# A hint for the closing branches of two hardware loops, in a fused attention and expert block

## The reference

```python
def _L0_attn_ref(x, w_kv_down, w_kv_up, w_q, w_out):
    kv = (x @ w_kv_down) @ w_kv_up
    ...
    att = jnp.einsum('bqhd,bkhd->bhqk', q, k) * scale
    att = jax.nn.softmax(jnp.where(causal, att, -jnp.inf), axis=-1)
    y = jnp.einsum('bhqk,bkhd->bqhd', att, v)
    return y.reshape(Bx, Tx, HD) @ w_out
...
    scores = jax.lax.stop_gradient(feats @ centroids.T)
    expert = jnp.argmax(scores, axis=1)
    alpha = jax.nn.sigmoid(jnp.sum(feats * centroids[expert], axis=-1, keepdims=True))
    ys = jax.vmap(_sublayer, in_axes=(None, 0, 0, 0, 0, 0, 0))(feats, gamma, beta, W1, b1, W2, b2)
    out = alpha * y + (1.0 - alpha) * feats
...
    x = x + _layernorm(_L0_attn_ref(_layernorm(x), ...))
    x = x + _layernorm(_L0_ffn_ref(_layernorm(x), ...))
```

## Time and profile before

| what | value |
|---|---|
| median of three runs | 1459.13 us (1459.09 to 1460.83) |
| profiled execution, its own time | 1459.58 us |
| span of its instructions | 1457.7 us |
| TensorE busy | 1343.0 us, 92% |
| VectorE busy | 1234.4 us, 85% |
| ScalarE busy | 1083.2 us, 74% |
| GpSimd busy | 809.8 us, 56% |
| mean granted TensorE clock | 0.977 |

### The profile page before, as it was taken

One profiled execution on the slowest core, in us unless ns is written; L12 is line 12 of the kernel. 1 busy time (PEld: TensorE's weight loads), 2 busy tenths in 40 slices (PEclk: granted clock), 3 DMA queues, 4 the chain that ended last, 5 costly groups with the idle time before them and its releaser, 6 DMA issues.

```text
span 1457.7 us, 34718 instructions
## 1 busy us (share of the span) xinstructions
PE 1343.0 (92%) x9120; PEld 1210.6 (83%) x9120; DVE 1234.4 (85%) x4806; ACT 1083.2 (74%) x3186; POOL 809.8 (56%) x1216
## 2 busy tenths in 40 slices
PE   7999999999999999999999999999999999599993
PEld 6988898888888988888888888888888888488872
DVE  5899888888888888888888888888888887499994
ACT  5888787878787878788787878787878886366661
POOL 3445555555555555555555555555555554178886
PEclk9999999999999999999999999999999999699997
DMA  4000000000000000000000000000000000312120
GB/s 194 5 9 12 12 11 12 11 8 11 12 11 12 11 11 10 9 11 11 11 11 12 11 10 11 10 11 12 11 12 11 9 9 14 95 48 63 59 62 8
DMA packets 38793, 32.39 MB, mean 22 GB/s; under 512 B 4882, under 2 KB 35990, under 8 KB 38304
## 3 DMA queue, kind: packets, MB, share of 16 engines
q1 hardware_dynamic: 31968, 21.61, 4.9%
q0 software_dynamic: 4608, 8.67, 1.7%
q10 hardware_dynamic: 2112, 1.11, 0.3%
HBM read 20.35 MB, written 12.07 MB: 22 GB/s over the span
## 4 chain that ended last, share of the span: by engine, by line
DVE 46%; issue 22%; ACT 18%; POOL 6%; PE 5%; ACTq 1%; DMA 1%; DVEq 1%; POOLq 0%; SPq 0%
DVE nscore L851 15%; DVE p_lo L861 13%; ACT prob L722 10%; ACT t_hi L694 5%; DVE nmax L851 2%; POOL prob L1037 2%; DVE ff L367 2%; DVE hitr L891 2%; DVE wup_s L384 1%; DVE on L393 1%; POOL pay L1056 1%; DVE fn L793 1%; DVE gg L402 1%; DVE t_lo L838 1%; DVE rinv L832 1%
## 5 line engine op out<-in xcount | busy, mean ns | idle before, releaser
L1037 POOL TENSOR_TENSOR prob<-prob,rinv 128x256 f32<-128x256 f32 (+1 forms) x512 | 413.2, 828 | 507.8 <-DVE rinv L832 507.7
L722 ACT ACTIVATE prob<-nscore,nmax 128x128 f32<-128x128 f32 (+1 forms) x1024 | 458.7, 449 | 248.4 <-DVE nmax L851 248.4
L851 DVE CUSTOM_DVE_ANT_0 nscore<-psS,mask 128x128 f32<-128x128 f32 (+1 forms) x1024 | 319.9, 350 | 0.0
L861 DVE TENSOR_TENSOR p_lo<-psP,p_hi 128x768 fp32r<-128x768 f32 x256 | 243.7, 952 | 1.0 <-ACT p_hi L694 0.9
L838 DVE TENSOR_TENSOR t_lo<-psT,t_hi 128x512 fp32r<-128x512 f32 x256 | 175.9, 687 | 56.0 <-ACT t_hi L694 56.0
L607 PE MATMUL psP<-ident,prob 128*128 128x128 f32 x1536 | 216.4, 277 | 6.8 <-DVE p_lo L861 6.7
L694 ACT ACTIVATE p_hi<-psP 128x768 fp32r<-128x768 f32 x256 | 204.9, 800 | 1.6 <-PE psP L607 1.6
L579 PE MATMUL psS<-t_lo,xt_hi 128*128 128x256 f32 (+1 forms) x512 | 196.8, 384 | 0.0
L722 ACT ACTIVATION_READ_ACCUMULATOR prob<-nscore,nmax 128x1 f32 x1024 | 191.3, 187 | 0.0
L607 PEld LDWEIGHTS psP<-ident,prob 128*128 128x128 f32 x1536 | 167.2, 141 | 22.7 <-POOL prob L1037 8.8
L867 DVE TENSOR_TENSOR z_lo<-psZU,z_hi 128x512 fp32r<-128x512 f32 x256 | 175.7, 686 | 3.3 <-ACT z_hi L694 3.3
(11 more groups left out here) (167 smaller groups left out, 3246.0 us busy)
## 6 DMA issues: line engine op xcount, KB each, us to landing
fin<-routed_rows SPq DMA_DIRECT2D x40, 136.0 KB, 2.2
wx<-ffn_w SPq DMA_DIRECT2D x2, 2058.0 KB, 12.0
xin<-x SPq DMA_DIRECT2D x32, 128.0 KB, 2.1
xres<-x SPq DMA_DIRECT2D x32, 128.0 KB, 2.1
out<-res,fin POOLq DMA_INDIRECT x80, 2.3
routed_rows<-padr ACTq DMA_DIRECT2D x4, 272.0 KB, 4.3
routed_rows<-padr SPq DMA_DIRECT2D x4, 272.0 KB, 5.4
wup_s<-wup SPq DMA_DIRECT2D x1, 1024.0 KB, 4.9
```

Source lines behind the costliest of these rows:

```text
L722: last = nc.scalar.activation(prob[:, p1, h, a:z], nscore[:, h, a:z], ACT.Exp, bias=nmax[:, p1, h, q:q + 1], scale=-1.0, accum_out=rsum[:, ...
L851: last = v.tensor_tensor_reduce(nscore[:, h, a:z], psQ[q][:, h, :], mask[:, a:z], -1.0, -MASKED, ALU.add, ALU.min, nmax[:, p1, h, q:q + 1])
L861: v.tensor_tensor(p_lo[:, (s - 3) % 2], psP[:, :, 0:384], p_hi[:, (s - 3) % 2].bitcast(F32), ALU.subtract).then_inc(S["p_split"], 1)
L1037: last = g.tensor_tensor(pr, pr, rinv[:, p2, :, q:q + 1].broadcast_to([P, 2, z - a]), ALU.mult)
```

## The change

Both loops are made through a small helper which asks for the same loop, on the same engine, with the option `hint_back_edge=True`.

```diff
+        def hinted_loop(eng, first, end):
+            return nc.Fori(first, end, engines=bass.OrderedEngineSet([eng.engine]), hint_back_edge=True)
+
         def ffn_phases(eng, slot):

             for s in range(FU):
                 slot(0, 0, s, lambda lag: s >= lag)
-            with eng.Fori(1, TILES // FU) as it:
+            with hinted_loop(eng, 1, TILES // FU) as it:
                 m0 = eng.snap(it * FU)
                 n0 = eng.snap(it * 16)
                 for s in range(FU):
@@ -476,7 +479,7 @@
             for s in range(SLOTS):
                 slot(0, 0, s, lambda lag: s >= lag, lambda d: s // PAIRS >= d)
             if ITERS > 2:
-                with eng.Fori(1, ITERS - 1) as it:
+                with hinted_loop(eng, 1, ITERS - 1) as it:
                     g0 = eng.snap(it * SLOTS)
                     b0 = eng.snap(it * 2)
                     for s in range(SLOTS):
```

## The result

| | before | changed |
|---|---|---|
| median | 1459.11 us (1458.6 to 1460.83, 4 runs) | 1434.78 us (1434.12 to 1435.53, 4 runs) |
| profiled execution, its own time | 1459.58 us | 1435.53 us |
| span | 1457.7 us | 1431.8 us |
| mean granted clock | 0.977 | 0.983 |

The profiled execution has 3.7 us around its span, that of before 1.9 (the other three runs of the change have 3.0, 2.0 and 2.0); what that is stays open. The ratio is 0.9831, with a 95% interval of 0.9814 to 0.9848: the change makes the kernel 24.3 us faster. Forecast were 1432.5 us, in a range of 1430.5 to 1439.0. The median is 2.3 us above the forecast, just outside the 1430.5 to 1434.5 that the forecast itself covered, and in the band of the rival *exits are paid* (1434.4 to 1438.2).

A forecast was written before the change was run, and what follows sets the result against it. It took the round VectorE, ScalarE and back as pacing the kernel, with VectorE idle for a code fetch at 13 attention edges. 1459.13 - 27.19 + 0.6 = 1432.5 us; range 1430.5 to 1439.

The forecast's parts named there:

- exits are paid: Rival: one to three late fetches behind a loop add 1.9 to 5.7 us, giving 1434.4 to 1438.2; chance 0.12.
- Step 1: Attention loop, VectorE's hint: the loop's head is fetched ahead, so 13 edges give back 27.19 us.
- ScalarE's wait for `nmax`: Sign in the attention loop: this wait falls by 13 x 1.9 = 25 us in all.
- The four dips of the clock inside the attention loop: Sign: the dips to 0.50, a second edge cost of 2.15 us within the 27.19, are gone.
- Step 2: Closing branch of the attention loop: about 0.46 us, covered by the 0.69 us last operation; cost 0.
- Step 3: One hint instruction per pass and engine: 0 in the attention loop, 0.6 us in the expert loop, at worst 1.3 there.
- Step 4: Leaving the loops, last branch falling through against its hint: taken as 0, at worst 5.7 us.
- Step 5: Expert loop's gain: no instruction packet there, so 0, at most 1.0 us.
- the hint does nothing: Rival: the fetch stays at all 13 attention edges, only 0.6 us is added, 1459.7 us; chance 0.09.
- works for half: Rival: the head is there but the next packet comes late, moving part of the stall into the pass; 1446 us; chance 0.03.
- drives out the fetches ahead: Rival: the fetcher holds to the loop's head, so four packets per attention pass are waited for; about 1540 us; chance 0.04.
- the useless fetch at the edge: Sign at the attention loop's edge: fewer instruction packets, since what is fetched in vain there is no longer.

The follow-up runs named there:

- a1: Kernel before plus the hint on VectorE's attention loop alone: 1432.95 us, ratio 0.9815 (kernel before on that chip 1460.75 us).
- a3: Kernel before plus the hint on the attention loop of TensorE, ScalarE, GpSimd and SyncE, not VectorE: 1460.7 us, ratio 1.0004.
- b1: Kernel before plus VectorE's attention hint alone, its outcome read from a register, not taken on the last pass: 1434.84 us, ratio 0.9818.
- c2: The changed kernel with every hint's outcome read from a register, not taken on a loop's last pass: 1432.80 us, ratio 0.9815 to the kernel before.
- c4: The same kernel as b1, run again on the chip shared with c1, c2 and c3: 1431.76 us, ratio 0.9815 to the kernel before.
- b2: Kernel before plus VectorE's attention hint alone, placed ahead of slot 15 instead of at the head of the pass: 1459.64 us, ratio 0.9996.
- a2: Kernel before plus the hint on all five engines' expert loops alone: 1462.35 us against 1460.75, ratio 1.0013.
- c1: The changed kernel itself, run again on one chip for comparison: 1434.46 us, ratio 0.9825 to the kernel before.
- c3: Kernel before plus the plain hint on VectorE's attention loop alone, same kernel as a1, rerun for comparison on one chip: 1434.53 us, ratio 0.983.

## Why the prediction was right, and where not

The mechanism of the gain was right and carries nearly all of the number. One term, put at 0, was wrong by 2.0 us; it came out within the range because its rival had been priced into it.

Step 1, the whole 27.19 us come back: 27.45 did, and all of it from VectorE (a1, a3). The other idle times at the edge were consequences of it, as the timelines had said; ScalarE's wait for `nmax` fell from 248.4 to 225.1 us, by 23 for the 25 forecast. The four dips of the clock inside the attention loop are gone with the stalls.

Step 2, the resident branch is covered: right, `an` starts 0.61 us behind the start of `z_lo`.

Step 3, the hint: mis-sized. I took 0.6 us in the expert loop; the issue waits ahead of `ff` went from 0.9 to 1.0 us in three edges, 0.33 at the first where I had looked for 0.4 to 0.6, and the three last passes take 102.00 us, beside 102.10 before. It costs 0.1 us or less in all. These 0.5 us too many offset a part of what step 4 missed; that is luck.

Step 4, leaving the loops, is the one that failed. I wrote that the fetch can begin at the branch at the latest, and took 0. It began when VectorE ran into the missing piece, 16 us behind the branch, so the wait was there in full: 1.92 us on VectorE, 2.00 on the pace. b1, c2 and c4 take it away by the outcome, and b2 shows that executing a hint asks for nothing. The cover that I gave was misread too: five packets in a pass are not five pieces of it. A pass is three pieces, and one lasts VectorE about 25 us (75.87 / 3), not 15. What I had as a rival, exits that are paid (1434.4 to 1438.2), is what happened: once, on VectorE behind the attention loop. TensorE's exit wait is hidden.

Step 5, no gain in the expert loop: right. Hints there alone even lost 0.13% (a2); within the whole change they were free (c1 beside c3).

Mended sum: 1459.13 - 27.45 + 2.0 + 0.1 = 1433.8; measured 1434.78. The rest of 1.0 us is open. In the spans of the two profiles it isn't there: 1457.7 - 27.45 + 2.0 + 0.1 = 1432.35, measured 1431.8. Nor is it the dip between the stages, which is 30.7 us in both. The profiled execution has 1.8 us more around its span than that of before, but two of the other three runs have 2.0 there, beside its 1.9.

Of the rivals, that the hint does nothing, works for half, or drives out the fetches ahead is excluded by the packets: none inside the loop. I had expected the useless fetch at the edge to go; all five went, by the picture above because with the first piece kept nothing was ever driven out. The Trainium skill, "Runtime: NRT & Kernel Launch", section Instruction fetch mechanics, calls fetching ahead purely sequential; without a hint that agrees with the five packets a pass, with the hint the measurement decides against it. It also says that a taken branch to code that isn't held waits for a fetch, and the trace agrees, with 2.25 us before and none when held.

## What to carry to other kernels

Look for issue waits whose count equals the number of taken back edges, with an instruction packet in them. Then hint that one loop of that one engine, at the head of the pass (27.45 us here), and say not taken on the last pass (about 2 us more). Or, if a pass just fits, put the loop's head at a piece's boundary; here that paid 2.7 us once, at the entry. Hints on the expert loop, which had nothing to fetch, gained nothing and alone cost 1.6 us (a2).

## What the runs showed of the hardware

- The code store of VectorE behaved as four pieces of 128 instructions: 384 instructions looped without a fetch when aligned (24 packets in the span) and with five fetches a pass when not (88). The number four is inferred from these two runs.
- A hint at the head of the pass took away 13 waits of 2.3 us; one 4.4 us ahead of the branch took away none, and no fetch followed on it. The packet that matters moved 10.3 us ahead of the branch.
- Behind a branch hinted as taken that fell through, the code was not fetched until it was needed: a wait of 1.9 to 2.1 us on VectorE, 16 us later.
- In the kernel before, four of the 13 stalls of 2.3 us on VectorE were followed by 3.4 us at half the granted clock (0.50), 0.5 us of time each. The dip to 0.50 between the stages was 27.3, 30.7 or 34.1 us long; the changed kernel had 30.7 and 27.3, the kernel of b1 and c4 34.1 and 27.3.
